# A mixture-of-experts block: the last expert in two halves, a second expert's rows placed later, and products of zeros between routing steps

## The chip, the cores and the metric

The kernel runs on one core of a Trainium2 chip. The metric is the time of one execution on the device in microseconds (us); less is better. The core has five engines with instruction streams of their own: TensorE (PE; its weight loads are shown as PEld), VectorE (DVE), ScalarE (ACT), GpSimd (POOL) and SyncE (SP). They wait for one another by semaphores, and here every order is written out by hand.

## The reference

The input is 4 x 1024 tokens of 128 numbers. After a modulated layer norm comes windowed attention (16 heads, 4 key and value heads, soft-capped scores) with a residual, then a second modulated layer norm and a mixture of experts with one expert per token:

```python
tokens = x.reshape(-1, H)                        # 4096 x 128
logits = tokens @ Wg                             # 8 experts
gates = softmax(logits); idx = argmax(gates)
mask1 = one_hot(idx, E)
locations1 = cumsum(mask1, axis=0) - 1.0         # place of the token with its expert
mask1 = mask1 * (locations1 < C)                 # C = 512 tokens for an expert
expert_in = dispatch(tokens)                     # 8 x 512 x 128
hidden = relu(expert_in @ W1 + b1)               # 8 x 512 x 512
expert_out = hidden @ W2 + b2                    # 8 x 512 x 128
out = gates1 * expert_out, back at the token; x = x + gb * out
```

## The kernel before

The 4096 tokens are 32 tiles of 128 (`TILES`; `LAST` is 31). The attention goes over the tiles in a software pipeline of all engines. Behind it each tile t passes a chain of small steps, the routing:

- `turn_y(t)` (TensorE) turns the attention's output; `add_x`, `measure2`, `gather2` (VectorE), `rstd2_of` (GpSimd), `normalise2`, `modulate2`, `shift2` (VectorE) make the residual and the second layer norm in a slot of `PAY`.
- `turn_h2(t)` (TensorE), `keep_h2(t)` (ScalarE) and `score_experts(t)` (TensorE) give the logits; `keep_logits`, `top8`, `which` (VectorE) and `mark(t)` (GpSimd, the one-hot) the expert.
- `count(t)` (TensorE), `locate(t)` (VectorE) and `number_slot(t)` (GpSimd) give the row in the sorted list, and `scatter(t)` (GpSimd, an indirect DMA) writes the token's row of 388 numbers to `sorted_rows` in DRAM.

SyncE waits for the scatters of tiles 0 to 29, then gathers the first 128 numbers of each row of experts 0 and 1 (line 351); the other numbers and the other experts' rows follow when the scatters of tiles 30 and 31 have landed, and these two scatters are held back until the first gathers have landed. What tiles 30 and 31 hold for experts 0 and 1 is added on TensorE instead: `spot(t)` (VectorE) builds a one-hot of 128 x 512 for each of the two experts, `place(t, e)` (line 717) multiplies it with the tile and accumulates into the bank `turn_banks[e]`, and `add_rows(e)` (line 722) adds the gathered rows by products with the identity.

Then the experts. Expert e has 512 rows. `turn_rows(e)` (line 742, from expert 2 on) transposes them into `turn_banks[e % 2]`; `high_rows(e)` (ScalarE, line 1059) and `low_rows(e)` (VectorE, line 1511) split them into a high and a low part, as `split_w1(e)` (line 1053) and `low_w1(e)` (line 1507) do with the weights. `up(e, f)` for f = 0 to 3 is three products of 512 columns (lines 386 to 388); `relu(e, f)` (ScalarE, line 1065) writes `hidden`. `down(e, s)` for s = 0 to 3 is four f32 products (line 762, eight instructions) into `down_banks[s % 2]`, one for 128 rows of the expert. It waits until the result two before it has been weighed: `weigh(e, s)` (line 1533) multiplies by the gate, `add_rest(e, s)` (line 1540) adds what `prepare(e)` (lines 1521 and 1524) made of bias and residual, `finish` is both, and `deliver(e, s)` (GpSimd, line 1810, an indirect DMA) writes 128 rows to the output.

## Time and profile before

| | before |
|---|---|
| median of 3 runs | 449.55 us (449.44 to 450.01) |
| the profiled execution | 448.8 us |
| its span | 447.1 us |
| busy in the span: PE, PEld | 94%, 66% |
| busy: DVE, ACT, POOL | 66%, 67%, 69% |
| mean granted clock of TensorE | 0.984 of full speed |

The span runs from the first to the last event of the profiled execution; the time has 1.7 us around it. Busy shares are means over stages: attention up to about 357 us, the last tiles' routing up to 379, the experts from there on. Full speed of TensorE's clock is 1.00; under 1.00 the throttle grants less.

### The profile page before, as it was taken

What the parts mean: (1) busy time and instruction counts of PE and PEld (TensorE: products, weight loads), DVE (VectorE), ACT (ScalarE), POOL (GpSimd) and SP (SyncE); (2) the same over time, 40 slices, a digit from 0 to 9 for tenths busy, and PEclk for the clock granted to TensorE, in tenths of its full rate; (3) what the DMA queues carried; (4) which work ended last, traced back from release to release, by engine and by line L of the source; (5) the groups of instructions that cost most, each with busy time, mean ns of one, the idle gap of its engine ahead of it and who ended that gap; (6) DMA issues with size and microseconds to landing.
All of it is one profiled execution on the core that took longest, in us unless ns stands there. A gap on an engine that the chain in (4) does not pass through costs nothing.

```text
span 447.1 us, 15012 instructions
## 1 busy us (share of the span) xinstructions
PE 421.4 (94%) x5630; PEld 294.0 (66%) x5630; DVE 294.5 (66%) x882; ACT 300.4 (67%) x537; POOL 310.4 (69%) x496
## 2 busy tenths in 40 slices
PE   8989999999999999999999999999998956989991
PEld 4756767666767676667666666767664643879991
DVE  6476576766786868566867674766668665476751
ACT  4987586868786868787868687776757433645540
POOL 4545575869887868687878777788668883175663
PEclk9999999999999999999999999999999995999998
DMA  8653702101110121021212201212021027594110
GB/s 245 227 182 133 214 9 78 36 23 37 38 50 27 49 63 32 20 79 38 60 39 68 67 14 38 61 38 79 21 67 50 25 60 220 200 369 164 33 43 28
DMA packets 33023, 37.15 MB, mean 83 GB/s; under 512 B 3650, under 2 KB 29255, under 8 KB 32952
## 3 DMA queue, kind: packets, MB, share of 16 engines
q1 hardware_dynamic: 29448, 27.43, 20.0%
q0 software_dynamic: 3072, 8.37, 5.1%
q8 instruction: 46, 0.75, 0.7%
q10 hardware_dynamic: 432, 0.40, 0.3%
q14 instruction: 25, 0.20, 0.2%
HBM read 15.69 MB, written 16.91 MB: 73 GB/s over the span
## 4 chain that ended last, share of the span: by engine, by line
PE 86%; DVE 3%; DMA 3%; issue 3%; POOL 2%; ACT 2%; POOLq 0%; SPq 0%; DVEq 0%; ACTq 0%
PE turns L498 13%; PE own L462 8%; PE turns L386 8%; PE turns L518 7%; PE turns L505 6%; PE turns L466 6%; PE turns L762 6%; PE turns L388 5%; PE turns L387 5%; PE turns L532 4%; PE turns L537 3%; PE turns L533 3%; PE own L455 2%; PE turns L544 1%; PE turns L394 1%
## 5 line engine op out<-in xcount | busy, mean ns | idle before, releaser
L1126 DVE COPY_PREDICATED own<-before,turns 128x1024 f32<-128x1024 uint32 x56 | 68.8, 1229 | 41.7 <-PE turns L466 41.7
L1641 POOL TENSOR_TENSOR OL<-O,OH 128x512 fp32r<-128x512 f32 x64 | 81.7, 1283 | 16.4 <-ACT OH L870 16.3
L857 ACT ACTIVATE PR<-own 128x1024 f32<-128x1024 f32 x64 | 65.4, 1022 | 15.6 <-DVE own L1126 15.6
L1632 POOL TENSOR_SCALAR_AFFINE_SELECT PM<-PR 128x1024 f32<-128x1024 f32 x64 | 70.2, 1098 | 7.4 <-ACT PR L863 7.1
L863 ACT ACTIVATE PR<-PR 128x1024 f32<-128x1024 f32 x64 | 67.2, 1050 | 0.1
L462 PE MATMUL own<-Q,K 64*32 64x128 f32 (+3 forms) x896 | 58.7, 441 | 2.7 <-issue 1.4
L466 PE MATMUL turns<-Q,K 64*32 64x128 f32 (+3 forms) x896 | 57.4, 429 | 0.0
L1159 DVE TENSOR_TENSOR O<-turns,R 128x512 f32<-128x512 f32 x64 | 43.0, 682 | 18.3 <-PE turns L505 18.2
L1686 POOL DMA_INDIRECT sorted_rows<-PAY,slot_i x32 | 34.7, 1083 | 17.7 <-issue 11.0
L466 PEld LDWEIGHTS turns<-Q,K 64*32 64x32 f32 x896 | 36.6, 107 | 9.5
L843 ACT ACTIVATE Q<-turns 128x512 f32<-128x512 f32 x64 | 38.3, 600 | 6.2 <-PE turns L388 5.0
L386 PE MATMUL turns<-XH,WqH 128*128 128x256 f32 x128 | 40.6, 318 | 0.0
L870 ACT ACTIVATE OH<-O 128x512 fp32r<-128x512 f32 x64 | 39.8, 625 | 0.3 <-DVE O L1159 0.3
L386 PEld LDWEIGHTS turns<-XH,WqH 128*128 128x128 f32 x128 | 24.6, 192 | 18.7 <-issue 9.5
L1065 ACT ACTIVATE PM<-turns,b_col 128x512 f32<-128x512 f32 x32 | 22.0, 688 | 22.1 <-PE turns L388 22.0
L387 PE MATMUL turns<-XL,WqH 128*128 128x256 f32 x128 | 36.1, 282 | 0.0
L388 PE MATMUL turns<-XH,WqL 128*128 128x256 f32 x128 | 36.0, 281 | 0.0
L498 PE MATMUL turns<-PR,V 128*32 128x256 f32 x448 | 35.1, 385 | 0.0
L498 PE MATMUL turns<-PR,VM 128*32 128x256 f32 x448 | 34.4, 379 | 0.0
L532 PE MATMUL turns<-OH,WoH 128*128 128x256 f32 x128 | 32.7, 294 | 0.3 <-DVE O L1159 0.3
L533 PE MATMUL turns<-OH,WoL 128*128 128x256 f32 x128 | 31.0, 281 | 0.0
L1646 POOL TENSOR_SCALAR var<-mv 128x1 f32<-128x1 f32 x32 | 6.1, 191 | 35.7 <-DVE mv L1178 34.3
(201 smaller groups left out, 1047.9 us busy)
## 6 DMA issues: line engine op xcount, KB each, us to landing
sorted_rows<-empty_row SPq DMA_DIRECT2D x8, 776.0 KB, 6.1
VM<-V SPq DMA_DIRECT2D x56, 64.0 KB, 2.1
out_dram<-PAY SPq DMA_DIRECT2D x32, 64.0 KB, 1.8
w_stage<-w_dram SPq DMA_DIRECT2D x8, 256.0 KB
PR<-sorted_rows SPq DMA_DIRECT2D x2, 776.0 KB, 8.6
x_sb<-sorted_rows SPq DMA_DIRECT2D x2, 776.0 KB, 11.1
x_sb<-x_dram SPq DMA_DIRECT2D x3, 512.0 KB, 5.9
O<-w_dram SPq DMA_DIRECT2D x4, 256.0 KB, 5.3
```

Source lines behind the costliest of these rows:

```text
L386: pe.matmul(dst, wh, xh, start=True, stop=False)
L387: pe.matmul(dst, wh, xl, start=False, stop=False)
L388: return pe.matmul(dst, wl, xh, start=False, stop=True)
L462: pe.matmul(own[lo:lo + B, a, :].rearrange("p (r n) -> p r n", n=P)[:, :, lo:P], keys(a, t, lo, lo + B), q(a, lo, P), start=True, stop=Tru ...
L466: last = pe.matmul(ps[lo:lo + B, a, :].rearrange("p (r n) -> p r n", n=P)[:, :, 0:lo + B], keys(a, t - 1, lo, lo + B), q(a, 0, lo + B), st ...
L498: last = pe.matmul(out_of(c, x, g), v[:, d], probabilities(PM if first(t) else PR, slice(0, P), g, c), start=(x == 0), stop=(x == 1 and fi ...
L532: pe.matmul(y, WoH[:, i, :], oh, start=(i == 0), stop=False)
L857: act.activation(pr, own[:, :, :].rearrange("p a n -> p (a n)"), ACT.Tanh, scale=SCORE_SCALE).then_inc(tanhed, 1)
L863: act.activation(pr, pr, ACT.Exp, scale=SOFTCAP).then_inc(exped, 1)
L1126: dve.copy_predicated(own[:, :, :].rearrange("p a (r n) -> p (a r) n", n=P), before[:, :].bitcast(U32).unsqueeze(1).to_broadcast([P, 2 * R ...
L1632: pool.affine_select(out=PM[:, u % P_RING, :].rearrange("p (r n) -> p r n", n=P), in_=PR[:, u % P_RING, :].rearrange("p (r n) -> p r n", n ...
L1641: pool.tensor_tensor(OL[:, t % 2, :, half], O[:, t % 2, :, half], OH[:, t % 2, :, half].bitcast(F32), ALU.subtract).then_inc(ol_done, 1)
```

## The change

There are four parts. In the TensorE stream `run_between(width)` multiplies zeros by zeros, `width` times 128 columns, into the bank `own`; ten such calls (of 1, 4, 2, 1, 4, 1, 4, 1, 3 and 4 units) stand between the steps of tiles 28 to 31, and the wait for all tanh comes ahead of the first. `place(LAST - 1, 1)` moves behind `add_rows(0)`, and `add_rows(1)` behind the second up product group of expert 0, with `high_rows(1)` on ScalarE behind the second relu. VectorE does `weigh(1, 0)` and `weigh(1, 1)` ahead of `low_w1(3)` and `prepare(1)`. And the last expert's up products and relus are made for 256 rows at a time, so that its down products of the first half need only the first half.

```diff
--- before.py
+++ after.py
@@ -572,6 +572,11 @@
                     pe.matmul(ps[:, 0:width * P].rearrange("p (a n) -> p a n", n=P), zeros[:, :],
                               zeros[:, :].unsqueeze(1).to_broadcast([P, width, P]), start=True, stop=True)
 
+            def run_between(width):
+
+                pe.matmul(own[:, 0, 0:width * P].rearrange("p (a n) -> p a n", n=P), zeros[:, :],
+                          zeros[:, :].unsqueeze(1).to_broadcast([P, width, P]), start=True, stop=True)
+
             pe.wait_ge(consts, 1)
             run_idle(2, 4)
 
@@ -695,21 +700,30 @@
             out_project(BLOCKS - 1)
             count(LAST - 4)
             turn_h2(LAST - 3)
+            pe.wait_ge(tanhed, 2 * TILES)
+            run_between(1)
             turn_y(LAST - 1)
             score_experts(LAST - 3)
+            run_between(4)
             turn_y(LAST)
+            run_between(2)
             count(LAST - 3)
             turn_h2(LAST - 2)
+            run_between(1)
             score_experts(LAST - 2)
+            run_between(4)
             turn_h2(LAST - 1)
+            run_between(1)
             score_experts(LAST - 1)
             count(LAST - 2)
+            run_between(4)
             turn_h2(LAST)
             count(LAST - 1)
+            run_between(1)
             score_experts(LAST)
-
-
-            pe.wait_ge(tanhed, 2 * TILES)
+            run_between(3)
+            run_between(4)
+
 
             def place(t, e):
                 pe.wait_ge(h2_done, t + 1)
@@ -724,11 +738,10 @@
 
             count(LAST)
             place(LAST - 1, 0)
-            place(LAST - 1, 1)
             place(LAST, 0)
             add_rows(0)
+            place(LAST - 1, 1)
             place(LAST, 1)
-            add_rows(1)
 
 
             for n in range(6):
@@ -751,6 +764,15 @@
                     pe.wait_ge(relu_done, FC * (e - 1) + f + 1)
                 three_passes(up_banks[f], w1H[:, e % 2, w], w1L[:, e % 2, w], xTH[:, e % 2, :], xTL[:, e % 2, :]).then_inc(up_done, 1)
 
+            def up_half(h, f):
+
+                e, w, at = EXPERTS - 1, slice(f * P, (f + 1) * P), slice(h * BT, (h + 1) * BT)
+                if h == 0 and f == 0:
+                    pe.wait_ge(xTL_kept, e + 1)
+                    pe.wait_ge(w1L_kept, e + 1)
+                pe.wait_ge(relu_done, FC * (e - 1 + h) + f + 1)
+                three_passes(up_banks[f][:, at], w1H[:, e % 2, w], w1L[:, e % 2, w], xTH[:, e % 2, at], xTL[:, e % 2, at]).then_inc(up_done, 1)
+
             def down(e, s):
                 n = ST * e + s
                 if s == 0:
@@ -759,12 +781,17 @@
                 if n >= 2:
                     pe.wait_ge(g_scaled, n - 1)
                 for f in range(FC):
+                    if e == EXPERTS - 1 and s == ST // 2:
+                        pe.wait_ge(relu_done, FC * (e + 1) + f + 1)
                     last = pe.matmul(down_banks[s % 2][:, 0:P], hidden[e % 2][:, f, s * P:(s + 1) * P], w2_sb[e][:, f, :],
                                      start=(f == 0), stop=(f == FC - 1))
                 last.then_inc(down_done, 1)
 
-            for f in range(FC):
-                up(0, f)
+            up(0, 0)
+            up(0, 1)
+            add_rows(1)
+            up(0, 2)
+            up(0, 3)
             up(1, 0)
             down(0, 0)
             up(1, 1)
@@ -783,19 +810,33 @@
             down(1, 3)
             up(2, 2)
             up(2, 3)
-            for e in range(3, EXPERTS):
+            for e in range(3, EXPERTS - 1):
                 up(e, 0)
                 down(e - 1, 0)
                 up(e, 1)
                 down(e - 1, 1)
                 up(e, 2)
-                if e < EXPERTS - 1:
-                    turn_rows(e + 1)
+                turn_rows(e + 1)
                 down(e - 1, 2)
                 up(e, 3)
                 down(e - 1, 3)
-            for s in range(ST):
-                down(EXPERTS - 1, s)
+
+            down(EXPERTS - 2, 0)
+            up_half(0, 0)
+            down(EXPERTS - 2, 1)
+            up_half(0, 1)
+            down(EXPERTS - 2, 2)
+            up_half(0, 2)
+            up_half(0, 3)
+            down(EXPERTS - 2, 3)
+            up_half(1, 0)
+            down(EXPERTS - 1, 0)
+            up_half(1, 1)
+            down(EXPERTS - 1, 1)
+            up_half(1, 2)
+            up_half(1, 3)
+            down(EXPERTS - 1, 2)
+            down(EXPERTS - 1, 3)
 
         def program_act(act):
             def split_high(i):
@@ -1064,15 +1105,24 @@
                 act.wait_ge(up_done, FC * e + f + 1)
                 act.activation(hidden[e % 2][:, f, :], up_banks[f], ACT.Relu, bias=b1_col[:, e, f:f + 1]).then_inc(relu_done, 1)
 
+            def relu_half(h, f):
+                e, at = EXPERTS - 1, slice(h * BT, (h + 1) * BT)
+                if h == 0 and f == 0:
+                    act.wait_ge(down_done, ST * (e - 1))
+                act.wait_ge(up_done, FC * (e + h) + f + 1)
+                act.activation(hidden[e % 2][:, f, at], up_banks[f][:, at], ACT.Relu, bias=b1_col[:, e, f:f + 1]).then_inc(relu_done, 1)
+
             act.wait_ge(w1_in, 16 * EXPERTS)
             act.wait_ge(rest_in, 32)
             act.wait_ge(masked, 2 * TILES)
             split_w1(0)
             split_w1(1)
             high_rows(0)
+            relu(0, 0)
+            relu(0, 1)
             high_rows(1)
-            for f in range(FC):
-                relu(0, f)
+            relu(0, 2)
+            relu(0, 3)
             relu(1, 0)
             split_w1(2)
             for f in range(1, FC):
@@ -1084,15 +1134,16 @@
             high_rows(3)
             relu(2, 2)
             relu(2, 3)
-            for e in range(3, EXPERTS):
+            for e in range(3, EXPERTS - 1):
                 relu(e, 0)
-                if e < EXPERTS - 1:
-                    split_w1(e + 1)
+                split_w1(e + 1)
                 relu(e, 1)
                 relu(e, 2)
-                if e < EXPERTS - 1:
-                    high_rows(e + 1)
+                high_rows(e + 1)
                 relu(e, 3)
+            for h in range(2):
+                for f in range(FC):
+                    relu_half(h, f)
 
         def program_dve(dve):
             def split_low(i):
@@ -1556,10 +1607,12 @@
             finish(0, 2)
             finish(0, 3)
             low_rows(2)
+            weigh(1, 0)
+            weigh(1, 1)
             low_w1(3)
             prepare(1)
-            finish(1, 0)
-            finish(1, 1)
+            add_rest(1, 0)
+            add_rest(1, 1)
             prepare(2)
             finish(1, 2)
             low_rows(3)
```

## Rows read from the trace of the kernel before

**Rows 1.** The chain of waits, 369 to 386 us: start us, us, what.

```profile
369.28 1.10 POOL sorted_rows L1686
...
370.48 0.31 POOL onehot L1657
...
371.92 4.03 DMA sorted_rows<-PAY,slot_i
...
376.15 2.88 DMA rows_at<-sorted_rows
...
379.08 1.16 PE own L722 x8
380.24 0.86 PE own L717 x2
...
382.82 2.73 ACT PM L1065 x4
```

**Rows 2.** Timeline of PE: start us, us, what, [idle before <-releaser].

```profile
363.38 0.36 PE L556 MATMUL turns<-Wg,h2T 128*128 128x8 f32 x2
364.80 0.33 PE L544 MATMUL turns<-ident,YT 128*128 128x128 f32 x1 [1.06 <-DVE PAY L1194]
...
368.15 0.45 PE L550 MATMUL turns<-ident,PAY 128*128 128x128 f32 x1 [1.14 <-DVE PAY L1194]
369.06 0.57 PE L556 MATMUL turns<-Wg,h2T 128*128 128x8 f32 x2 [0.46 <-ACT h2T L886]
...
370.79 0.45 PE L550 MATMUL turns<-ident,PAY 128*128 128x128 f32 x1 [1.12 <-DVE PAY L1194]
```

**Rows 3.** Windows: length, PE busy, granted clock, DMA; the last with all engines.

```profile
367.50:368.00 0.50, 0.00 (x0) 0.64 0.75 156
...
377.50:378.00 0.50, 0.50 (x2) 0.62 0.89 209
...
442.00:443.00 1.00, 0.00 (x0) 0.00 (x0) 0.00 (x0) 0.00 (x0) 0.00 (x0) 0.87 0.17 50
```

**Rows 4.** Timeline of PE, the placing products.

```profile
374.47 4.50 PE L717 MATMUL own<-PM,PAY 128*128 128x512 f32 x6
```

**Rows 5.** Timeline, expert 0: first weight load, high part, first down product.

```profile
381.82 0.19 PEld L386 LDWEIGHTS turns<-xT,WqH 128*128 128x128 f32 x1
...
382.03 0.60 ACT L1059 ACTIVATE xT<-own 128x512 fp32r<-128x512 f32 x1 [1.16 <-PE own L722]
...
385.60 1.16 PE L762 MATMUL turns<-O,PM 128*128 128x128 f32 x8
```

**Rows 6.** Timeline, expert 1.

```profile
392.61 0.69 DVE L1511 TENSOR_TENSOR xT<-own,xT 128x512 fp32r<-128x512 f32 x1 [0.45 <-ACT xT L1059]
...
395.49 1.16 PE L762 MATMUL turns<-O,PM 128*128 128x128 f32 x8 [1.05 <-DVE R L1533]
```

**Rows 7.** Timeline, low rows of expert 3 and the down products of expert 2.

```profile
398.60 0.69 DVE L1511 TENSOR_TENSOR xT<-own,xT 128x512 fp32r<-128x512 f32 x1 [0.37 <-ACT xT L1059]
...
400.86 1.16 PE L762 MATMUL turns<-O,PM 128*128 128x128 f32 x8
```

**Rows 8.** Timeline: out_project's products, a copy of 256 columns, the end.

```profile
360.76 0.28 PE L532 MATMUL turns<-OH,WoH 128*128 128x256 f32 x1
360.88 0.28 PE L533 MATMUL turns<-OH,WoL 128*128 128x256 f32 x1
...
362.32 0.47 ACT L880 ACTIVATE YT<-turns,ga_col 128x256 f32<-128x256 f32 x1 [1.08 <-PE turns L537]
...
431.01 0.97 POOL L1810 DMA_INDIRECT out_dram<-sumsT,x_sb  x1 [0.55 <-issue]
...
432.94 4.78 PE L762 MATMUL turns<-VD,PM 128*128 128x128 f32 x40
...
436.72 0.97 POOL L1810 DMA_INDIRECT out_dram<-R,OH  x1 [0.30 <-DVE R L1540]
...
440.55 0.97 POOL L1810 DMA_INDIRECT out_dram<-R,OH  x1 [0.30 <-issue]
```

## The prediction

> **What bounds the kernel now.** I read the page first. TensorE is busy 94% of the span and nearly always at full clock, so over the 360 us of attention nothing but TensorE's own work counts, and the change leaves that alone. It touches three places in the last 85 us, where the reader should look at who waits for whom.
>
> First place, the routing of the last tiles. The chain of waits [rows 1] goes over GpSimd (the one-hot of tile 30), then 4.03 us of landing for the scatter of tile 29, then 2.88 us in which SyncE's gather of expert 0's rows lands at 379.0. TensorE is only a passenger between 363 and 379: it has ten short steps, separated by waits of 0.4 to 1.1 us [rows 2]. Its granted clock falls from 1.00 (2.4 GHz) to 0.50 (1.2 GHz) at 367.7, 5.2 us after its dense work ended at about 362.5, and comes back at 377.9, 3.4 us after the placing products began at 374.5 [rows 3, 4]. After the last product of the kernel the clock falls 5.1 us later again (end 437.7, fall 442.8) [rows 3, 8].
>
> Second place, the start of the experts. From 379.1 TensorE, ScalarE (high part), VectorE (low part) form a relay; then ScalarE's four relus, back to back from 382.82 to 385.55, hold up the first down product until 385.60, after 0.52 us idle [rows 1, 5]. At expert 1 the third down product stands still for 1.05 us until 395.49, because the bank it needs is freed by a weighing that VectorE does behind the low rows of expert 2, the low weights of expert 3 and two steps of preparing [rows 6].
>
> Third place, the end. From 431.0 GpSimd issues the last eight deliveries. The last four start between 436.72 and 440.55, thus 1.277 us apart with a gap of 0.30 after each, which is GpSimd's own pace and not TensorE's [rows 8]. The span ends 5.6 us after the last of them, landing included.
>
> **The change part by part.** The sum is made against the profiled execution, 448.8 us (span 447.1 and 1.7 around it); the median of the runs is 449.55, so 0.75 above it.
>
> *Products of zeros.* A 512-column f32 product is two instructions; at full clock two such instructions take 0.86 us [rows 1], at the low one 1.72 (six took 4.50 us, the clock rising ahead of the last ones) [rows 4]. The insertions have 25 units of 128 columns, so 25 x 0.215 = 5.4 us at full clock. Each lies in a wait. The four units after score_experts(28) run from about 363.6 to 364.5, and the next step can't go before 364.8. The four after score_experts(29), from 367.0 to 367.9, end before the second layer-norm of tile 30 is there (368.15 in the trace, at most 0.15 sooner). The four after count(29) end by 370.4, against 370.8. The seven after score_experts(31) end by 373.9; count(31) is at 374.2, behind GpSimd's one-hot. The single ones fall into the 0.4 us in which ScalarE copies h2T. The added wait for all tanh is long over (the last attention product is at 357). So they cost 0, at most 0.15. What do they give? With the clock up, the two turns and two scores at the low clock shorten by 0.12 and 0.2 each [rows 2]. But the one-hot of tile 30 starts at 370.48 right behind a scatter on GpSimd (369.28 + 1.10) and can gain only 0.1 [rows 1]. I take 0.05, between 0 and 0.1. The rest of the chain is DMA.
>
> *Placing order.* With the clock up, place(30,0) and place(31,0) need 1.72 us from 374.5 (VectorE has the last one-hots at 375.1) and end at 376.2. TensorE is then idle for 2.85 us until the rows land. place(30,1) and place(31,1) come behind add_rows(0): add_rows(0) issues in 0.89 us to 379.97, four instructions in 1.72 to 381.8. Before, two of them (0.86) and add_rows(1) (0.89) stood there, and the first up began at 381.8 [rows 1, 5]. VectorE's low part is ready at 381.6. Same start, to 0.05.
>
> *add_rows(1) behind up(0,1), and high_rows(1) behind relu(0,1).* Here I expect a loss. TensorE: two ups from 381.8 to 383.3 (0.77 and 0.68), add_rows(1) 0.89 to 384.15, two ups to 385.5 with their last result at about 385.8. ScalarE: relu(0,0) and relu(0,1) from 382.8 to 384.2, high_rows(1) 0.60 at about 384.4, relu(0,2) at 385.1, relu(0,3) from 385.8 to 386.5 [rows 1, 5]. up(1,0) is ready behind VectorE's low part at 385.7. So the first down product starts at 386.5 instead of 385.6: plus 0.9. The bound from below is ScalarE alone, four relus and one copy from 382.8, 386.15: plus 0.55. TensorE then carries the delay to turn_rows(2) (391.35 becomes 392.2).
>
> *Weighing sooner.* weigh(1,0) and weigh(1,1) now come right behind low_rows(2). That one starts 0.9 later too, at 393.5, and ends at 394.2; weigh(1,0) is done at 394.5. TensorE does the two down products of expert 1 and up(2,0) until 395.1 and goes on with down(1,2) without waiting, at 395.1 instead of 395.49. Next late is VectorE: from low_rows(2) to low_rows(3) it has 398.60 - 392.61 = 5.99 us with 0.37 idle, hence 5.6 us of work, less 0.1 for the paired steps [rows 6, 7]. low_rows(3) then starts at 393.5 + 5.5 = 399.0, ends at 399.7, and up(3,0) follows at 399.8 (399.92 before). The other branch is up(2,3), 0.35 sooner, relu(2,3) 0.35 sooner, and down(2,0), which waits for it, starts at 400.5 instead of 400.86 [rows 7]. Both parts of the start together: minus 0.3, within minus 1.2 (no loss at add_rows(1)) and plus 0.5 (nothing given back). After 400.9 TensorE has no gap for 37 us, so this goes through. The rows of expert 3 must be there by 396.7; TensorE took them at 397.2 without waiting.
>
> *The last expert by halves.* The trace of before has no three-pass product of 256 columns with expert weights, but out_project's alternate two weight sets on 256 columns at 0.12 us each [rows 8]. A half is 3 x 0.12 = 0.36 against 0.345 for half of a whole, so eight cost 0.1 us more. The upper bound takes the weight load's 0.19 [rows 5] for every pass: 24 x 0.07 = 1.7 us. I take 0.1, since the row has the same shape. ScalarE's eight half relus cost about 0.47 each (128x256 from PSUM [rows 8]), 1.0 us more in all, hidden since it rests there over a third of the time. The down products of expert 6 now start right behind down(5,3), at 427.4, so those of expert 7 finish between 433.8 and 437.6 rather than between 434.8 and 437.7. From a down product's end to its delivery go 1.65 us, so the four could start at 435.4, 436.7, 438.3 and 439.2. GpSimd decides: delivery (6,0) stays at 431.01, because VectorE prepares expert 7 before it, and seven steps of 1.277 end in 439.95 instead of 440.55. Minus 0.6. The bounds are 0 (the pace slips) and minus 0.9.
>
> Sum: -0.05 - 0.3 - 0.6 = -0.95, in the profile's terms 447.85 us. For the median I would add 0.75 back, 448.6. Yet this profile is one in which the clock came back 1.1 us before the rows landed. Had it come back later, TensorE would have started the experts at half speed, and part of the 0.75 may be just that; the change spares it if the clock never falls. Halfway: **448.3 us**.
>
> **The rivals.**
> *The clock falls in the new gap.* TensorE's wait for the rows grows from nothing to 2.85 us. For it: at 367.7 the clock fell though short products ran in the wait before. Against it: both falls came more than 5 us after dense work had ended, and the stalls of up to 1.5 us later on cost nothing. If it falls as the rows land and stays low as long as after 374.5, 3.4 us, half of that is lost: +1.7, so 449.5 in the profile's terms and 449.5 to 450.3 as a median, no difference. If it stays low through the first expert, 6 us from 379, it costs 3.0: 450.8 to 451.6, slower. It decides from a loss of 1.9 on. The Trainium skill, "TensorE: Matmul & The Clock Gate", section "HAM oscillation — how this bites in real kernels", tells of just this, a burst of products that waits for a DMA and starts cold each time; by that rule the time would be the one of this rival, and no row of before has a wait of this length to test it.
> *Nothing is given back at expert 1,* since expert 1's or 3's rows land later than I think, or VectorE stays behind: +0.9 instead of -0.3, -0.05 and -0.6 stay, 449.05, as a median 449.4 to 449.8, no difference.
> *The end gains nothing,* because half products go at the weight load's pace or the deliveries wait: -0.35 in all, 448.5 to 449.2.
> *The zeros don't keep the clock up.* They fill about half of 363 to 374. Then each four-unit product takes 1.72 and outlasts its wait by 0.2 to 0.7, the scatter of tile 29 moves by about 0.2, and the dense zeros behind score_experts(31) bring the clock back before 379: -0.7, 448.1 to 448.9.
>
> **How the numbers follow.** Forecast 45%; gap short 14%, gap long 9%; expert 1 gives nothing 11%; end gives nothing 12%; zeros without effect 9%. What a measurement can tell from no change is 0.2% or 0.9 us, thus below 448.65 or above 450.45. The forecast case (447.4 to 448.9) is faster in four of five (0.36), the case of the end in one of three (0.04), that of the zeros in three of four (0.07); the long gap is the slower one (0.09). With 0.03 more for faster and 0.04 for slower, for effects that I don't see: faster 0.50, same 0.37, slower 0.13. The range goes from 447.0 (the loss at add_rows(1) smaller) to 450.5.
>
> **What would show it.** The granted clock 1.00 from 363 to the end of the products; if it is 0.5 anywhere from 379 to 385, the gap rival holds. First down product about 0.9 later than the rows' landing plus 6.56 us. No wait at down(1,2), low_rows(3) as the last condition of up(3,0). Last delivery 0.6 us nearer to the start of expert 6, at a pace of 1.277. The prediction is wrong if the rows' landing itself moves by over 0.3 us, or if the half products cost more than 0.15 us per pass.

## The result, and the profile after

The changed kernel takes 450.52 us (447.23 to 452.46, 22 executions); the kernel before, on the same chip and in the same rounds, 448.37 us (447.84 to 450.01, 22). The ratio is 1.0034 with a 95% interval of 1.0021 to 1.0047: slower by about 1.5 us, where 0.9 us can be told from no change. The ratio is taken over the executions; the two medians alone stand 2.15 us apart (1.0048). An execution over 1.5% above the fastest of its kernel counts as slow and is left out of the ratios: none here, three in one kernel below. The profiled execution took 450.05 us with a span of 448.3 us, against a span of 447.1 before.

From the profile page of the kernel after: the span, the busy times of the engines (share of the span, instructions), and the clock that TensorE was granted, in 40 slices.

```profile
span 448.3 us, 15080 instructions
PE 426.0 (95%) x5662; PEld 296.9 (66%) x5662; DVE 294.1 (66%) x882; ACT 301.3 (67%) x541; POOL 310.3 (69%) x496
PEclk8999999999999999999999999999999998899997
```

The granted clock still has a dip near slice 34, where the zeros should have taken it away. The chain of waits of the kernel after (start us, us, what) shows what stands there:

```profile
371.12 4.14 DMA sorted_rows<-PAY,slot_i
375.47 2.98 DMA rows_at<-sorted_rows
378.49 2.07 PE own L736 x8
380.56 3.41 PE own L731 x4
...
396.77 0.29 DVE R L1584
```

Up to the landing little has changed from [rows 1]: from ScalarE's copy of YT (361.56) to the scatter of tile 29 it takes 9.56 us instead of 9.60, and the two transfers are as long as before within 0.2 us. But add_rows(0), now at line 736, takes 2.07 us where it took 1.16, and the four placing instructions behind it 3.41. The timeline of TensorE in the kernel after:

```profile
373.16 1.95 PE L731 MATMUL own<-PM,PAY 128*128 128x512 f32 x4
378.49 2.07 PE L736 MATMUL own<-ident,rows_at 128*128 128x128 f32 x8 [3.38 <-DMA rows_at<-sorted_rows]
380.35 3.62 PE L731 MATMUL own<-PM,PAY 128*128 128x512 f32 x4
382.99 1.42 PE L386 MATMUL turns<-xT,WqH 128*128 128x512 f32 x1
...
388.67 1.09 PE L786 MATMUL turns<-O,PM 128*128 128x128 f32 x8
...
397.27 1.05 PE L786 MATMUL turns<-O,PM 128*128 128x128 f32 x8
...
402.02 0.50 PE L386 MATMUL turns<-xT,WqH 128*128 128x512 f32 x1 [0.29 <-DVE xT L1562]
```

And its windows over the wait (length, PE busy, granted clock, DMA share and GB/s):

```profile
364.00:374.90 10.90, 9.11 (x38) 1.00 0.67 223
374.90:377.50 2.60, 0.21 (x1) 0.99 0.32 63
377.50:378.50 1.00, 0.01 (x1) 0.50 1.12 334
...
384.00:384.50 0.50, 0.50 (x3) 0.72 0.00 0
384.50:385.00 0.50, 0.50 (x4) 1.00 0.00 0
```

So the zeros did what they should: the clock was 1.00 from 364 on, where it was 0.50 from 367.7 before [rows 3], and the first placing products took 1.95 us for four. But then TensorE stood still for 3.38 us, the clock fell to 0.50 (1.2 GHz) at 377.5, one microsecond ahead of the rows, and came back at 384.3. The experts' start, 6 us of dense work on the path, ran at half speed. The first up product starts 4.50 us after add_rows(0) (2.77 before: its first product is at 381.85, behind the weight load of [rows 5]), the first down product 10.18 us after it (6.52 before).

Two later rows answer to [rows 6, 7]: down(1,2) at 397.27 no longer waits, and what holds up(3,0) at 402.02 for 0.29 us are the low rows. In the chain of waits, VectorE is what counts from the weighing at 396.77, its last line above, up to those low rows. At the end four rows of the kernel after answer to [rows 8]: two half passes of an up product, and the last four deliveries, from first to last.

```profile
435.85 0.28 PE L387 MATMUL turns<-xT,WqH 128*128 128x256 f32 x1
435.97 0.29 PE L388 MATMUL turns<-xT,WqL 128*128 128x256 f32 x1
...
437.96 0.97 POOL L1863 DMA_INDIRECT out_dram<-R,OH  x1 [0.30 <-DVE R L1591]
...
441.80 0.97 POOL L1863 DMA_INDIRECT out_dram<-R,OH  x1 [0.30 <-issue]
```

The ledger of the profiled execution against the one before: attention ended 0.76 us sooner, which the change doesn't touch; the routing up to the scatter -0.04; scatter to add_rows(0) +0.21 (7.37 for 7.16); from there to the high rows of expert 7 +2.45 (48.70 for 46.25); from those to the last delivery -0.61 (14.61 for 15.22); the end -0.05. The sum is +1.2, the difference of the spans. The whole loss, and more, is made from add_rows(0) on, in the start of the experts: 2.25 of the 2.45 us are there at the high rows of expert 3.

The other executions say how often. Their mean granted clock falls in two groups with nothing between. In 17 of 22 it is 0.986 or lower, and they take 450.05 to 452.46 us, median 450.7. In 5 it is 0.989 or higher, and they take 447.23 to 448.76, median 448.0. A clock of half for 6.8 us takes 3.4/448 = 0.0076 from the mean, about the distance of the two groups' middles (0.984 and 0.991). The mean alone doesn't name the stretch: the profile of the changed kernel has a second one at half clock, near the start of the attention (0.50 from 9 to 12 us, the 8 in its first slice), which the profile before hasn't. But the times part too, with nothing between 448.76 and 450.05. So the clock probably fell in the wait in about three of four executions, and by this reading, not shown by a trace, the change would have gained 0.4 us without it.

### The profile page after: what moved, and what is told of

The parts are those of the page before. It is cut to its first block, busy times and chain, and to the rows that moved or that the text cites. A ratio compares the mean times of both kernels' runs of the same rounds, so it can differ in the third digit from the quotient of the medians.

```text
span 448.3 us, 15080 instructions
## 1 busy us (share of the span) xinstructions
PE 426.0 (95%) x5662; PEld 296.9 (66%) x5662; DVE 294.1 (66%) x882; ACT 301.3 (67%) x541; POOL 310.3 (69%) x496
## 4 chain that ended last, share of the span: by engine, by line
PE 87%; DVE 4%; issue 2%; DMA 2%; POOL 2%; ACT 1%; POOLq 0%; DVEq 0%; ACTq 0%; SPq 0%
PE turns L498 13%; PE own L462 8%; PE turns L386 8%; PE turns L518 7%; PE turns L505 6%; PE turns L786 6%; PE turns L466 6%; PE turns L388 5%; PE turns L387 5%; PE turns L532 4%; PE turns L537 3%; PE turns L533 3%; PE own L455 2%; PE turns L544 1%; PE turns L394 1%
## 5 line engine op out<-in xcount | busy, mean ns | idle before, releaser
L1106 ACT ACTIVATE PM<-turns,b_col 128x512 f32<-128x512 f32 x28 | 19.2, 688 | 20.9 <-PE turns L388 20.8
```

## The experiments

All ratios are against the kernel before on the same chip, with 95% intervals. The kernel before itself had a median of 448.37 us on the chip of the result, but 453.26, 452.67, 453.63 and 452.84 in the four series below. "Start" is the time from add_rows(0) to the first up product and to the first down product in the profile; "tail" the time from the high rows of expert 7 to the last delivery. Before: 2.77 and 6.52; 15.22. The four series ran on chips numbered 9, 8, 2 and 2; each kernel has 12 executions (10 of the changed kernel again) and one profile. Where an interval includes 1, the time shows no difference, and only the profile speaks.

### Is it the clock, and who makes it fall

**The wait filled.** Eight more instructions of zeros behind place(31,0), adding zeros to the open sum of expert 0:

```diff
             place(LAST, 0)
+            for _ in range(4):
+                pe.matmul(turn_banks[0].rearrange("p (a n) -> p a n", n=P), zeros[:, :],
+                          zeros[:, :].unsqueeze(1).to_broadcast([P, 4, P]), start=False, stop=False)
             add_rows(0)
```

> The changed kernel with four more products of zeros (512 columns each, added to the bank of expert 0 without changing it; 3.44 us at full clock) between place(31,0) and add_rows(0), where the changed kernel waits for 3.38 us and its clock falls. Theory 1 (the clock that falls in this wait costs the time): the clock stays at 1.00 through the experts, the first down product comes 7.4 us after the rows' landing instead of 10.3, and the median is 0.3 to 1.0 us below before. Theory 2 (the later add_rows(1) costs it, the clock is incidental): the clock stays up, but the median stays 1 us or more above before. If the zeros outlast the wait, up to 0.3 us is lost with both.

Timeline of TensorE in this kernel:

```profile
377.90 3.60 PE L743 MATMUL own<-zeros 128*128 128x512 f32 x8
382.62 1.16 PE L736 MATMUL own<-ident,rows_at 128*128 128x128 f32 x8 [1.12 <-DMA rows_at<-sorted_rows]
383.61 1.88 PE L731 MATMUL own<-PM,PAY 128*128 128x512 f32 x4
385.39 0.47 PE L386 MATMUL turns<-xT,WqH 128*128 128x512 f32 x1
```

The clock stays at 1.00, add_rows(0) is back at 1.16 us and the first up product at +2.77, the first down product at +7.49. The start is what the forecast said it would be. Yet the kernel is not faster: 1.0027 [1.0001, 1.0054]. Here the last expert loses time that the first profile of the changed kernel doesn't lose (tail 16.94); it is taken up below. This profile has one more stretch at clock 0.50, from 338.7 to 342.1, in the attention, where the edit does nothing; so have those of the kernel without zeros and of the one with all half up products ahead.

**The change without its zeros**, the rest kept:

```diff
-            run_between(1)
...
-            run_between(3)
-            run_between(4)
```

> The changed kernel without its ten products of zeros. Theory 1: the clock falls at some time between 364 and 371 as in before; the two placings ahead of the rows run slow and end 0.3 to 1.1 us ahead of the landing, and since they are all the dense work by then, the clock is often still low when the rows land: between before and the changed kernel, +0.5 to +1.5 us against before. Theory 3 (the zeros themselves delay the routing): 1 us or more faster than the changed kernel, and the scatter of tile 29 is issued sooner than in it.

1.0015 [0.9993, 1.0036], tail 18.02. The clock is 0.50 from 370 to 380, the placing before the landing takes 3.68 us instead of 1.95 and so ends 1.03 us before the rows are there; the clock is up when they come, and the start is +2.77 and +7.50.

**The zeros alone**, in the kernel before with its placing order:

```diff
+            pe.wait_ge(tanhed, 2 * TILES)
+            run_between(1)
             turn_y(LAST - 1)
             score_experts(LAST - 3)
+            run_between(4)
...
+            run_between(3)
+            run_between(4)
```

> Before with only the ten products of zeros and the earlier wait for tanh. The three placings ahead of the rows run at full clock and leave a wait of about 2.5 us. Theory 1: the clock falls in this wait in a part of the executions, fewer than in the changed kernel; median +0.5 to +1.5 us against before, with executions at a high clock (0.989 or more) equal to before within 0.5 us. Theory 2: equal to before, within 0.4 us. Theory 3: +1 us or more in all executions alike.

Timeline of TensorE in this kernel:

```profile
375.27 2.81 PE L731 MATMUL own<-PM,PAY 128*128 128x512 f32 x6
381.65 1.71 PE L736 MATMUL own<-ident,rows_at 128*128 128x128 f32 x8 [3.58 <-DMA rows_at<-sorted_rows]
```

1.0022 [0.9996, 1.0048]. With the clock up, six placing instructions take 2.81 us, TensorE waits 3.58 us, and the clock falls at 382.1, 0.4 us after add_rows(0) has begun, and is back at 385.5; the start is +4.33 and +8.14. So in this profile the order of placing isn't needed for the fall; the zeros alone make it. Without them the slow clock stretched the placing over the wait, which brought the clock back about when the rows landed.

**The price of the fall alone.** Two kernels without the halves of the last expert, on one chip, that differ only in the eight instructions that fill the wait:

The first, against the changed kernel:

```diff
-            for e in range(3, EXPERTS - 1):
+            for e in range(3, EXPERTS):
...
-            down(EXPERTS - 2, 0)
-            up_half(0, 0)
...
+            for s in range(ST):
+                down(EXPERTS - 1, s)
...
-            for h in range(2):
-                for f in range(FC):
-                    relu_half(h, f)
```

> The changed kernel with the last expert whole again (zeros, placing order, later add_rows(1), sooner weighing stay). It is free of the stop in the last expert, so it shows the rest of the change. Theory 1: the clock falls in the wait for the rows in most executions, the experts start with it at 0.50, and the median is +1 to +2 us against before.

The second is the same with the four 512-column products of zeros behind `place(LAST, 0)`, as above.

> The one before with four products of zeros (3.44 us) in the wait for the rows; nothing else differs. Theory 1: the clock stays up, and it is 1.5 to 2.5 us faster than e13 in the same call, -0.5 to -1 us against before. Theory 2 (the clock is incidental): equal to e13 within 0.5 us.

The timeline of TensorE in the one whose wait is empty, and its windows:

```profile
381.81 2.07 PE L736 MATMUL own<-ident,rows_at 128*128 128x128 f32 x8 [4.38 <-DMA rows_at<-sorted_rows]
383.68 3.20 PE L731 MATMUL own<-PM,PAY 128*128 128x512 f32 x4
```

```profile
378.00:379.00 1.00, 0.00 (x0) 1.00 0.00 0
379.00:380.00 1.00, 0.00 (x0) 0.75 0.08 9
380.00:381.00 1.00, 0.00 (x0) 0.50 0.92 228
```

And of the one whose wait is filled:

```profile
376.75 3.60 PE L743 MATMUL own<-zeros 128*128 128x512 f32 x8
381.45 1.16 PE L736 MATMUL own<-ident,rows_at 128*128 128x128 f32 x8 [1.10 <-DMA rows_at<-sorted_rows]
382.44 1.88 PE L731 MATMUL own<-PM,PAY 128*128 128x512 f32 x4
```

Empty: 453.40 us, 1.0009 [0.9984, 1.0035]. Filled: 451.35 us, 0.9964 [0.9939, 0.9989]. The difference of the medians, 2.05 us, is the price of the fall; the two intervals together leave it at 2.0 us give or take 1.6. In the profiles the high rows of expert 3 come 21.46 us after add_rows(0) in the empty one and 18.81 in the filled one, 2.65 us apart; at expert 7 it is 1.63, because between experts 3 and 4 the filled one takes 8.16 us and the empty one 7.18, a delay that is taken up at the end. The filled one, all parts but the halves, has the lowest ratio of the kernels made from these parts.

### The two shifts at the start of the experts

**add_rows(1) and high_rows(1) later, alone**, in the kernel before:

```diff
-            add_rows(1)
...
-            for f in range(FC):
-                up(0, f)
+            up(0, 0)
+            up(0, 1)
+            add_rows(1)
+            up(0, 2)
+            up(0, 3)
...
+            relu(0, 0)
+            relu(0, 1)
             high_rows(1)
-            for f in range(FC):
-                relu(0, f)
+            relu(0, 2)
+            relu(0, 3)
```

> Before with only add_rows(1) behind up(0,1) and high_rows(1) behind relu(0,1). By my prediction the first down product is 0.9 us later (0.55 at least) and most of it comes through, since the third down product of expert 1 waits for VectorE whatever TensorE does: +0.5 to +0.9 us. Theory 2 wants +1.5 us or more. If it is 0 or less, the later add_rows(1) costs nothing, and my sum had a wrong sign there.

The first down product starts 7.62 us after add_rows(0): +1.1 us, where the forecast had +0.9. A part of it is the clock, which came back only at 380.9 here, 0.5 us into add_rows(0), so that the first up product is at +2.90; in the three kernels with the moves and the clock up it is 7.48 to 7.50, +1.0 us for the two moves. At the high rows of expert 3 all of it is still there (19.96 for 18.90). 1.0022 [0.9996, 1.0047], with medians of 453.16 and 453.26: the loss stands in the profile and isn't shown in the time.

**Weighing sooner, alone**, in the kernel before:

```diff
             low_rows(2)
+            weigh(1, 0)
+            weigh(1, 1)
             low_w1(3)
             prepare(1)
-            finish(1, 0)
-            finish(1, 1)
+            add_rest(1, 0)
+            add_rest(1, 1)
```

> Before with only weigh(1,0) and weigh(1,1) ahead of low_w1(3) and prepare(1). By my sum the third down product of expert 1 stops waiting (1.05 us in before), turn_rows(3) comes 1.0 to 1.3 us sooner after the landing, and VectorE's own work lets 0.3 to 1.1 us of it through to expert 3's turn_rows(4): median -0.3 to -1.1 us. A rival is that the rows of expert 1 or 3 come too late for it: 0.

0.9973 [0.9949, 0.9997], 1.2 us faster. The high rows of expert 3 come 18.13 us after add_rows(0) instead of 18.90: 0.77 us of it is seen there. The interval overlaps with that of the filled kernel, so which of the two is the faster is not shown.

Both together, with the clock up, are in the filled kernel above: high rows of expert 3 at +18.81, 0.1 sooner than before.

### The last expert by halves

**The halves alone**, in the kernel before: `up_half`, `relu_half`, the waits in `down(7, 2)` and the written-out order of the diff of the change, and nothing else of it but the earlier place of the wait for all tanh, which is long over there:

```diff
+            down(EXPERTS - 2, 0)
+            up_half(0, 0)
...
+            up_half(1, 0)
+            down(EXPERTS - 1, 0)
...
-            for s in range(ST):
-                down(EXPERTS - 1, s)
```

> Before with only the last expert's up products and relus by halves. By my sum the last delivery comes 0.6 us nearer to the start of the last expert: median -0.6 us. The two profiles of kernels with halves just taken (e1 and e2) show something new there, a stop of ScalarE and once of VectorE of 2.1 to 3.1 us in the last expert that no engine or known queue ends. If the longer ScalarE program brings it (theory 4), it shows here too, and the median is +1 to +2 us instead; if it belongs to these two executions alone, the profile has none and the median is -0.6.

1.0035 [1.0018, 1.0052], slower by 1.6 us; the tail is 17.69 instead of 15.22. The timeline of its last expert, with all engines (PE line 777 is a down product, ACT 1101 a half relu, DVE 1570 a weighing):

```profile
435.73 1.05 PE L777 MATMUL turns<-VD,PM 128*128 128x128 f32 x8
...
437.22 0.28 PE L388 MATMUL turns<-xT,WqL 128*128 128x256 f32 x1
437.34 0.60 PE L777 MATMUL turns<-VD,PM 128*128 128x128 f32 x4
...
439.60 0.29 DVE L1570 TENSOR_TENSOR R<-turns,OH 128x128 f32<-128x128 f32 x1 [2.82 <-remote]
439.65 0.84 ACT L1101 ACTIVATE PM<-turns,b_col 128x256 f32<-128x256 f32 x2 [3.13 <-remote]
...
440.17 2.87 PE L777 MATMUL turns<-VD,PM 128*128 128x128 f32 x12 [2.23 <-ACT PM L1101]
...
442.78 0.97 POOL L1847 DMA_INDIRECT out_dram<-R,OH  x1 [0.80 <-DVE R L1577]
...
444.49 0.97 POOL L1847 DMA_INDIRECT out_dram<-R,OH  x1 [0.74 <-DVE R L1577]
```

Windows of TensorE over the same stretch:

```profile
439.00:440.00 1.00, 0.00 (x0) 1.00 0.20 66
440.00:441.00 1.00, 0.83 (x4) 0.70 0.00 0
441.00:442.00 1.00, 1.00 (x7) 0.50 0.00 0
```

The down product of 435.73 has its modelled end at 436.78 and the last up pass at 437.50; VectorE and ScalarE get to work on them only at 439.60 and 439.65. "remote" names no instruction of the core as the one that released them. With the halves TensorE waits for that relu inside its down product, 2.2 us; the clock falls once more, at about 440.4, the deliveries come 1.7 us apart instead of 1.28. The same stop stands in the profiles of the kernels with the wait filled and without zeros, on another chip, but not in the first profile of the changed kernel.

**The changed kernel again**, unedited, on the chip of the halves alone.

> The changed kernel once more, on the chip of the other three, for its profile beside theirs. Theory 1: the clock falls in the wait for the rows in most executions, and the first down product comes 9 to 10.5 us after the landing; +1 to +2.5 us against before. Theory 4: in the last expert the same stop as in the halves alone.

1.0065 [1.0041, 1.0090]. Start +4.50 and +10.16 as on the first chip, clock 0.50 when the rows land; but the tail is 17.68, not 14.61. The loss is the fall and the stop together.

**Wait filled, halves, and the old order of expert 1's rows** (high_rows(1) too stands where it did before), against the changed kernel:

```diff
             place(LAST - 1, 0)
+            place(LAST - 1, 1)
             place(LAST, 0)
+            for _ in range(2):
+                pe.matmul(turn_banks[0].rearrange("p (a n) -> p a n", n=P), zeros[:, :],
+                          zeros[:, :].unsqueeze(1).to_broadcast([P, 4, P]), start=False, stop=False)
             add_rows(0)
-            place(LAST - 1, 1)
             place(LAST, 1)
+            add_rows(1)
...
-            add_rows(1)
```

> The changed kernel with the old order at expert 0 (three placings ahead of add_rows(0), place(31,1) and add_rows(1) right behind it, high_rows(1) ahead of the relus) and two products of zeros (1.72 us) in the wait for the rows. Theory 1: the clock stays at 1.00, the first down product comes 6.5 us after the landing as in before, and with weighing and halves the median is 1.0 to 1.8 us below before. Theory 2 says the same. With theory 4 it is 1 to 2 us worse than that.

1.0028 [1.0003, 1.0054]. Clock up over a wait of 1.83 us, first down product at +6.52, thus the +1.0 of the moves is gone, and the stop in the last expert (tail 17.25) keeps the kernel above the one before.

**What of the halves makes the stop.** First the kernel before again, unedited.

> The kernel before, as a control: the ratio shows what the comparison calls a difference where there is none (expected 0.998 to 1.002), and the profile shows whether before, too, has the stop in the last expert on these chips. Theory 4 (the halves bring it): no stop. Theory 5 (it comes in part of the executions of any kernel): perhaps one here.

1.0001 [0.9978, 1.0024], tail 15.31.

The down products of expert 6 one place sooner, all products whole, in the kernel before:

```diff
-            for e in range(3, EXPERTS):
+            for e in range(3, EXPERTS - 1):
...
+            down(EXPERTS - 2, 0)
+            up(EXPERTS - 1, 0)
+            down(EXPERTS - 2, 1)
+            up(EXPERTS - 1, 1)
+            up(EXPERTS - 1, 2)
+            down(EXPERTS - 2, 2)
+            up(EXPERTS - 1, 3)
+            down(EXPERTS - 2, 3)
```

> Before with only the order of the last expert's part of the halves: each down product of expert 6 ahead of the up product that stood before it, ups and relus whole (512 columns). It tells the order from the half instructions. Theory 4a (the half products or half relus bring the stop): no stop, time equal to before within 0.3 us. Theory 4b (the order brings it): stop, +1 to +2 us.

0.9991 [0.9969, 1.0013], tail 15.35: the order alone brings neither a stop nor a loss that can be seen.

Whole up products, but eight half relus, in the kernel before:

```diff
...
+            for f in range(FC):
+                for h in range(2):
+                    relu_half(h, f)
```

> Before with only expert 7's relus by halves on ScalarE, eight instead of four, in the old order; TensorE's products are whole. ScalarE's program is as long as with the full halves. Theory 4c (the longer ScalarE program brings the stop, by the fetch of instructions or otherwise): stop of 2 to 3 us between the seventh and eighth of them or near, +1 to +2 us. Else no stop; the down products of expert 7 start later by about 0.25 us since the last relu pair takes 0.84 instead of 0.69.

1.0004 [0.9977, 1.0032], tail 15.90, 0.6 longer, but without the stop: the last relu is where it was, 7.81 us after the high rows of expert 7.

The kernel before with the zeros, two filling products before `add_rows(0)` and the sooner weighing, no halves:

```diff
+            for _ in range(2):
+                pe.matmul(turn_banks[0].rearrange("p (a n) -> p a n", n=P), zeros[:, :],
+                          zeros[:, :].unsqueeze(1).to_broadcast([P, 4, P]), start=False, stop=False)
             add_rows(0)
...
```

> Before with weighing sooner, the ten products of zeros, and two more of 512 columns in the wait for the rows; no halves, old order at expert 0. If theory 1 (clock) and theory 4 (halves) are the two things that cost: clock 1.00 through the experts, no stop, 1.0 to 1.8 us below before. If it is not below e5 (weighing alone, 0.9973), the zeros give nothing.

1.0005 [0.9972, 1.0039] from nine executions (450.4 to 456.2 us; the three left out go up to 460.1), clock up over a wait of 0.54 us, no stop (tail 15.37). With this spread it is inconclusive: it doesn't bear out the sum of its parts, and doesn't refute it.

The halves with one wait in `down(7, 2)` in place of four, the rest as in the kernel before:

```diff
-                    if e == EXPERTS - 1 and s == ST // 2:
-                        pe.wait_ge(relu_done, FC * (e + 1) + f + 1)
+                    if e == EXPERTS - 1 and s == ST // 2 and f == 0:
+                        pe.wait_ge(relu_done, FC * (e + 2))
```

> The halves alone, with one wait for all four relus at down(7,2) instead of one for each of its products. Theory 6 (the four waits, close behind one another on TensorE, bring the stop): no stop, -0.3 to -0.6 us against before. If it isn't the waits, the stop of 2.4 us stays, +0.35% like e6.

1.0050 [1.0021, 1.0079], with the stop (3.11 us on ScalarE, 2.79 on VectorE, both "remote"), tail 19.02: not the four waits.

All half up products ahead of `down(7, 0)`, the rest as in the kernel before:

```diff
...
+            up_half(0, 0)
+            up_half(0, 1)
+            down(EXPERTS - 2, 1)
+            up_half(0, 2)
+            up_half(0, 3)
+            down(EXPERTS - 2, 2)
+            up_half(1, 0)
+            up_half(1, 1)
+            down(EXPERTS - 2, 3)
+            up_half(1, 2)
+            up_half(1, 3)
...
```

> The halves alone, with all eight half up groups ahead of the first down product of expert 7, so that no half product stands among them. Theory 7 (half products of the second half between the down products of expert 7 bring the stop): no stop, time equal to before within 0.4 us (the deliveries of expert 7 come as late as in before). If half products bring it wherever they stand, the stop stays.

1.0016 [0.9986, 1.0045], tail 16.78. ScalarE is no longer stopped, but the first weighing is, in the timeline of this kernel:

```profile
438.19 1.95 PE L777 MATMUL turns<-VD,PM 128*128 128x128 f32 x16
...
440.95 0.29 DVE L1568 TENSOR_TENSOR R<-turns,OH 128x128 f32<-128x128 f32 x1 [2.65 <-PE turns L777]
```

So results come late at this place in both orders of the halves, and in none of the kernels without them is the last relu late (7.8 to 7.9 us after the high rows in each, 12.8 to 13.5 in the six with the stop; with halves and no stop, in the first profile of the changed kernel, it is 10.4). Why they come late is open, see below.

## Why the prediction was wrong

Forecast 448.3 us, faster with 0.50; measured 1.0034, slower, to which I gave 0.13.

**The failed step is the weighing of "the clock falls in the new gap".** I saw the gap, gave it 2.85 us (it is 3.38) and two prices, +1.7 and +3.0, but only 23% together, on the ground that "both falls came more than 5 us after dense work had ended" [rows 3, 8]. Both were readings of a clock after dense attention or expert work. Nothing in them says how long it stays up after the routing, where TensorE is busy 9.11 of 10.90 us with short steps and zeros, and then has nothing. There the clock fell 2.4 us after the last placing product, and 2.1 us after it in the kernel without halves. For the start of the experts up to expert 3 my sum had -0.3, and the profile has +2.25. The price was right: 2.05 us measured between the two kernels that differ by this alone, between my two cases, which met the point "from 1.9 on". The rule of the Trainium skill that I had set beside it, "TensorE: Matmul & The Clock Gate", section "HAM oscillation — how this bites in real kernels", that a burst of products that waits for a DMA starts cold each time, spoke for the rival. The trace agrees with it: the clock was 0.50 when the rows landed, in both profiles of the changed kernel, behind waits of 3.38 and 4.30 us.

**I treated the low clock before as pure cost.** In the first profile of the kernel before it did work: slow placing products, 4.50 us for six [rows 4], filled the wait for the rows and brought the clock back 1.1 us before they landed. The zeros took this away and put nothing in its place; with the zeros alone the clock falls at the landing. The text said that the change "spares" the risk of a late clock, when it made that risk the rule. The risk itself was real: in four later profiles with the placing of before, all six placing products run at the low clock, and the kernel with the down products sooner shows what comes of it:

```profile
375.09 5.46 PE L717 MATMUL own<-PM,PAY 128*128 128x512 f32 x6
380.34 1.16 PE L722 MATMUL own<-ident,rows_at 128*128 128x128 f32 x8
```

Its weight load for add_rows(0), which waits for the rows, is at 379.55, so the product at 380.34 comes 0.8 us late; in the other three it is 0.4 to 0.5, and the first down product is late by up to 0.2 more. So there was something to gain, but the fall costs more.

**Products of zeros: 0, gain 0.05.** Right: 0.04 in the routing. That they fill "about half" was right too: 5.78 of the 10.90 us from 364 to 374.9 are products of zeros, and with the steps between them TensorE is busy for 9.11. The clock stayed at 1.00.

**add_rows(1) and high_rows(1): +0.9.** Measured +1.0 with the clock up (+1.1 alone, with a late clock), and right in kind: the first down product waits for ScalarE's relus.

**Weighing sooner: -0.3 for both together.** Right in sign: -0.77 alone at the high rows of expert 3 and -0.1 for both together with the clock up. down(1,2) goes on without waiting, and the low rows are the last condition of up(3,0), as said.

**The halves: -0.6.** Right in the first profile, where the tail is 14.61 for 15.22, with half passes at 0.12 us (435.97 less 435.85), half relus at 0.47 and GpSimd's 1.28 as the pace. On another chip wrong in sign: the halves alone cost 1.6 us. I had "the end gains nothing" at 12%, with late deliveries as one of its causes, and no case in which it loses.

The range, 447.0 to 450.5, ends where the measured median of 450.52 stands, but on a chip where before has 448.37 and not 449.55, so the change itself is further off than that. Of the 0.75 between the profiled execution and the median of three I gave half back, as perhaps the clock's; with 22 executions the median is 448.37, 0.4 below the profiled one, so the 0.75 was the spread of three.

**What stays open.** On the chip of the result I have one profile of the changed kernel, without the stop; that its other executions lose by the clock is read from their mean clock, not from a trace. And the cause of the late results in the last expert was not found. Each by itself, the sooner down products, half relus with whole up products and the zeros don't bring it, and it stays without the four waits. Nor does a transfer of instructions that the profile shows fall into it: from 434 to 440, around the stop of the kernel with the halves alone, only the queue of the deliveries has packets. What is left is half up products, for a reason that no run tells, and they don't bring it every time: the first profile of the changed kernel has them and no stop. The kernel before has such lateness too, at another place: between the high rows of experts 3 and 4 it took 9.24 us on the chip of the third series, 6.95 in the first profile, and 6.5 to 8.8 in the other kernels. The timeline of ScalarE there, in the kernel before run again, and the same relus in the first profile:

```profile
399.25 0.59 ACT L1059 ACTIVATE xT<-own 128x512 fp32r<-128x512 f32 x1
402.93 2.00 ACT L1065 ACTIVATE PM<-turns,b_col 128x512 f32<-128x512 f32 x3 [3.10 <-PE turns L388]
```

```profile
399.43 2.14 ACT L1065 ACTIVATE PM<-turns,b_col 128x512 f32<-128x512 f32 x3 [0.86 <-PE turns L388]
```

ScalarE waits 3.10 us for the same up product for which it waited 0.86 us in the first profile. Such a delay costs its own length where all work is in line. My guess, argued and not shown, is that the halves make their one dearer, since TensorE then stands idle and restarts at the low clock, while whole products had all been issued.

## What to carry to other kernels

A filler that keeps the clock up has to reach to the end of the wait, not only to the last step before it: faster work in front of a transfer makes a longer empty wait behind it, and what counts is the clock at the landing. Ask of each slow stretch what its slowness covers, before removing it. And after the parts of a change are costed, run each without the others: here two (weighing sooner, -0.27%; the wait filled, 2.05 us) carried a faster kernel, 0.9964, that two others (the halves, the empty wait) hid. On the chip of the result this kernel was not run.

## What the runs showed of the hardware

- The granted clock fell from 1.00 to 0.50 in waits of 3.38, 4.30 and 4.38 us behind the routing, and 0.4 us after the end of one of 3.58; it stayed up where zeros cut the wait to 0.54, 1.10, 1.12 and 1.83 us. At the low clock eight 128-column instructions took 2.07 us instead of 1.16. It came back 5.8 us after add_rows(0) had begun (378.49 to 384.3) and 4.5 in the kernel without halves (381.81 to 386.3), longer than the 3.4 us in [rows 4].
- The same kernel has a median of 448.37 us in the series of the result and 452.67 to 453.63 in four series on chips 9, 8 and 2, about 1% more, with 2.3 us more between two experts in one profile there. The number of the first chip isn't known, so that the chip makes the difference is likely and not shown.
- TensorE's results can reach the other engines 2 to 3 us after the modelled end of their products (439.60 for 436.78), with the granted clock at 1.00 and no instruction named as the releaser.
